# Two half-buffers that each carry four whole batches, at a shift, in a two-layer attention kernel on one core

## The reference

```
def half_ffn(x):                      # layer 0, before and after attention
    x = x + 0.5 * (gelu(LN(x) @ U1 @ V1 + b1) @ U2 @ V2 + b2)
def attn0(x):                         # 16 heads of 8, causal, softmax
    p = softmax(mask(q @ k.T / sqrt(8)));  return LN(p @ v) * gamma + beta @ Wo
def moe(x):                           # layer 1, before and after attention, halved
    shared = silu(x @ sw1) * (x @ sw3) @ sw2
    routed = sum over the 2 best of 8 experts of gate * (gelu(x @ ew1[e]) @ ew2[e])
def attn1(x):                         # 16 heads, features of 16, values of 64, causal
    w = mask(1 + s + s*s/2)           # s = q.k/4, a Taylor series of exp
    return (w @ v) / sum(w) @ Wo
layer: x -> + ffn/2 -> + attn(LN(x)) -> + ffn/2
```

## Time and profile before

| | us |
|---|---|
| median of 3 runs (range) | 1528.44 (1524.53 to 1531.28) |
| the profiled execution's own time | 1527.06 |
| its span, first to last instruction | 1525.3 |
| mean granted TensorE clock | 0.937 of full |
| PE / VectorE (DVE) / ScalarE (ACT) / GpSimd (POOL) busy | 1249.5 / 1078.3 / 757.7 / 307.8 |

### The profile page before, as it was taken

How to read it: one execution, slowest core, us unless ns; L and a number is a source line. 1 busy time by engine, 2 the same in 40 slices (tenths; PEclk the granted TensorE clock), 3 DMA queues, 4 the chain that set the end, 5 groups by cost and what they waited for, 6 DMA issues and landing times. The chain is left out here.

```text
span 1525.3 us, 30378 instructions
## 1 busy us (share of the span) xinstructions
PE 1249.5 (82%) x10040; PEld 687.8 (45%) x10064; DVE 1078.3 (71%) x3235; ACT 757.7 (50%) x1251; POOL 307.8 (20%) x807
## 2 busy tenths in 40 slices
PE   5598659888798877888789887888778889898886
PEld 3254235445443454435454344543445335554544
DVE  6985378667786678856788657876687667776756
ACT  3166336652566435664266532765327663454442
POOL 1024001430014200242002420123101331022220
PEclk8799779998899988999889997999979999999999
DMA  3100000000010000100001000010000100101000
GB/s 114 42 2 1 7 21 22 23 8 22 10 37 7 8 26 6 43 2 11 27 2 43 8 10 21 2 43 8 17 13 1 43 1 2 43 8 43 1 2 14
DMA packets 37243, 29.20 MB, mean 19 GB/s; under 512 B 7960, under 2 KB 36304, under 8 KB 37072
## 3 DMA queue, kind: packets, MB, share of 16 engines
q1 hardware_dynamic: 37072, 27.04, 6.6%
HBM read 5.90 MB, written 2.10 MB: 5 GB/s over the span
## 5 line engine op out<-in xcount | busy, mean ns | idle before, releaser
L772 ACT ACTIVATE left<-bank 128x512 f32<-128x512 f32 x280 | 160.6, 601 | 86.3 <-PE bank L1242 83.8
L814 ACT ACTIVATE right<-bank 128x512 f32<-128x512 f32 x280 | 158.6, 602 | 88.5 <-PE bank L1329 81.5
L962 DVE TENSOR_REDUCE left<-bank 128x4 f32<-128x512 f32 x280 | 184.5, 682 | 22.0 <-PE bank L1223 21.0
L1221 PE MATMUL bank<-left 128*128 128x512 f16 (+1 forms) x448 | 130.2, 341 | 67.0 <-DVE left L952 29.9
L1165 PE MATMUL bank<-right,pairs 128*128 128x512 f16 x588 | 167.9, 410 | 20.1 <-DVE right L1041 11.9
L1092 DVE TENSOR_SCALAR right<-right 128x1024 f32<-128x1024 f32 x168 | 105.7, 655 | 64.9 <-ACT right L814 63.7
L1062 DVE SCALAR_TENSOR_TENSOR right<-bank,right 128x128 f32<-128x128 f32 x448 | 125.9, 343 | 30.2 <-PE bank L1305 26.1
L1355 PE MATMUL bank<-right 128*32 128x256 f32 (+3 forms) x1792 | 133.1, 435 | 0.0
L1305 PE MATMUL bank<-ew,right 128*128 128x128 f32 x896 | 119.7, 278 | 10.0 <-ACT right L791 5.7
L1305 PEld LDWEIGHTS bank<-ew,right 128*128 128x128 f32 x896 | 113.4, 191 | 30.5 <-ACT right L791 11.2
L1242 PE MATMUL bank<-left 128*128 128x512 f16 (+1 forms) x448 | 102.4, 304 | 16.8 <-DMA left<-left 8.9
(11 more groups left out here) (281 smaller groups left out, 2289.8 us busy)
## 6 DMA issues: line engine op xcount, KB each, us to landing
right<-right SPq DMA_DIRECT2D x168, 64.0 KB, 2.1
left<-left SPq DMA_DIRECT2D x168, 32.0 KB, 1.9
left<-x_dram SPq DMA_DIRECT2D x7, 256.0 KB, 2.8
out_dram<-right SPq DMA_DIRECT2D x7, 256.0 KB, 2.5
left<-left SPq DMA_DIRECT2D x24, 64.0 KB, 2.1
right<-right SPq DMA_DIRECT2D x24, 32.0 KB, 1.9
wo<-wo_dram SPq DMA_DIRECT2D x1, 512.0 KB, 3.5
ew<-ew_dram SPq DMA_DIRECT2D x1, 512.0 KB, 4.2
```

The lines of the kernel that those rows point to most:

```text
L772: act.activation(h.probs[:, g % 2, u * S:(u + 1) * S], ps[:, :], ACT.Exp).then_inc(h.act, 1)
L814: act.activation(h.wts[:, p % 2, u * S:(u + 1) * S], ps[:, :], ACT.Square, bias=1.0, scale=FEAT ** -0.5).then_inc(h.act, 1)
L962: dve.tensor_reduce(h.bmax[:, u * NT:(u + 1) * NT], ps[:, :].rearrange("p (b k) -> p b k", k=P), AX.X, ALU.max).then_inc(h.dve, 1)
L1221: mm(ps[:, c0:c0 + n_keys], h.q0a[:, g, qt * P:(qt + 1) * P], h.kpad0[:, g * GH + j, 0:n_keys], start=True, stop=False)
```

## The change

- **Sections.** Each half now carries four whole batches, each as attention and then Taylor: left the even ones (A1, B1), right the odd ones (A2, B2). The right starts when the left has got to `exp 13` of its first attention, and keeps that distance. The body holds a whole batch of each half and is written out three times; there is no hardware loop, and all waits are on constants. At the end the left finishes first and the right's last Taylor stream goes on alone from its seventh square.
- **Hand-over.** `take` and its two buffers are gone, since a half's Taylor stream reads the x that its attention stream left. The next x is loaded (`fetch`) after the first expert of the second feed-forward. The result has a buffer of its own.
- **LayerNorm.** The centring moves from VectorE to GpSimd: with shift = -mean * rstd, four `tensor_scalar` (x * rstd + shift), after two small multiplies and one more tiny addition that carries a wait.
- **Taylor weights.** GpSimd masks first, with -1 as fill, then adds one over the whole stretch of 1024 or 512 columns; VectorE has no part in it.
- **Values.** ScalarE evacuates both banks.

```diff
-SECTIONS = {
-    "begin": {"L": listing(("A1", 0, ORDER_A), ("A1", 1, FRONT)), "R": listing(("A2", 0, ORDER_A))},
-    "body": {"L": listing(("A1", 1, BACK), ("A1", 2, FRONT)), "R": listing(("B2", 0, ORDER_B))},
-    "finish": {"L": listing(("A1", B - 2, BACK), ("B1", 0, ORDER_B)),
-               "R": listing(("B2", B - 3, ORDER_B), ("B2", B - 2, ORDER_B))},
-}
-TURNS = B - 3
+    expert.8 fetch expert.9-15 store""")
+
+BATCH = [("A", step) for step in ORDER_A] + [("B", step) for step in ORDER_B]
+LEFT_CUT, RIGHT_CUT = BATCH.index(("A", "exp 13")), BATCH.index(("A", "stat 0"))
+TURNS = B // 2 - 1
+
+
+def span(side, first, last, turn):
+
+    return [(kind + side, turn, step) for kind, step in BATCH[first:last]]
+
+
+def sections(left, right):
+
+    n = len(BATCH)
+    return {
+        "begin": {"L": span("1", 0, left, 0), "R": span("2", 0, right, 0)},
+        "body": {"L": span("1", left, n, 0) + span("1", 0, left, 1), "R": span("2", right, n, 0) + span("2", 0, right, 1)},
+        "finish": {"L": span("1", left, n, TURNS), "R": span("2", right, n, TURNS)},
+    }
+
+
+SECTIONS = sections(LEFT_CUT, RIGHT_CUT)
 
...
     if name == "v1":
-        return [("low", "act"), ("high", "dve")]
+        return [("low", "act"), ("high", "act")]
...
-        def run(eng, fns, engine):
-
-            steps(fns, 0, "begin", engine)
-            with eng.Fori(0, TURNS) as i:
-                steps(fns, i, "body", engine)
-            steps(fns, 0, "finish", engine)
+        def run(eng, fns, engine, enter=None):
+
+            steps(fns, 0, "begin", engine, enter)
+            for i in range(TURNS):
+                steps(fns, i, "body", engine, enter)
+            steps(fns, 0, "finish", engine, enter)
...
                   .then_inc(h.res_free, 16)
 
-            def load_next(h, it, _n, step):
-                if not (isinstance(it, int) and it == 0):
-                    load(h, it, _n, step)
-
-            run(sp, dict(load=load_next, qkv0=qkv0, shift=shift, qk1=qk1, store=store), "sp")
-            sp.wait_ge(B2.res_free, 16 * B)
-            sp.wait_ge(B1.res_free, 16 * 2)
+            def fetch(h, it, _n, step):
+                if isinstance(it, int) and it == TURNS:
+                    return
+                sp.wait_ge(h.moe_added, (it * 2 + 1) * (NE + 1) + 1)
+                load(h.partner, it + 1)
+
+            run(sp, dict(fetch=fetch, qkv0=qkv0, shift=shift, qk1=qk1, store=store), "sp")
+            for h in (B1, B2):
+                sp.wait_ge(h.res_free, 16 * (B // 2 + 1))
...
@@ -673,8 +678,20 @@
             def ln_scale(h, it, k, step):
                 pool.wait_ge(h.mv_ready, it * h.lns + k + 1)
                 pool.tensor_tensor(h.vare[:, :], h.mv[:, :, 1], epsilon[:, :], ALU.add).then_inc(h.vare_ready, 1)
+                pool.tensor_tensor(h.shift[:, :], h.mv[:, :, 0], minus[:, :], ALU.mult)
                 pool.wait_ge(h.vare_ready, it * h.lns + k + 1)
                 pool.tensor_tensor(h.rstd[:, :], h.vare[:, :], neghalf[:, :], ALU.pow).then_inc(h.rstd_ready, 1)
+                pool.wait_ge(h.rstd_ready, it * h.lns + k + 1)
+                pool.tensor_tensor(h.shift[:, :], h.shift[:, :], h.rstd[:, :], ALU.mult).then_inc(h.shift_ready, 1)
+                pool.wait_ge(h.shift_ready, it * h.lns + k + 1)
+                pool.tensor_tensor(h.spare[:, :], neghalf[0:1, 0:1], neghalf[0:1, 0:1], ALU.add)
+                src = h.attn if h in (A1, A2) and k == 2 else h.x
+                for t in range(NT):
+                    last = pool.tensor_scalar(h.ln[:, t, :], src[:, t, :], h.rstd[:, t:t + 1], h.shift[:, t:t + 1],
+                                              ALU.mult, ALU.add)
+                last.then_inc(h.ln_ready, 1)
+                if h in (A1, A2) and k == 0:
+                    pool.memset(h.vaug[:, :, :, HD0:HD0 + 1], 1.0).then_inc(h.ones_laid, 1)
 
             def wait_apart(h, it, n, sem, value):
 
...
                     k = p * NC + list(COMPLETE1).index(u)
-                    wait_apart(h, it, k, h.plus1, it * NPAIR * NC + k + 1)
-                for kt in COMPLETE1.get(u, ()):
-                    mask(h.wts[:, p % 2, :], 2, kt).then_inc(h.masked1, 1)
+                    wait_apart(h, it, 2 * k, h.act, drained(h, it, step, "s"))
+                    for kt in COMPLETE1[u]:
+                        last = mask(h.wts[:, p % 2, :], 2, kt, -1.0)
+                    last.then_inc(h.cut1, 1)
+                    wait_apart(h, it, 2 * k + 1, h.cut1, it * NPAIR * NC + k + 1)
+                    v = h.wts[:, p % 2, (u // 2 * 2) * S:(u + 1) * S]
+                    pool.tensor_scalar(v, v, 1.0, 1.0, ALU.mult, ALU.add).then_inc(h.masked1, 1)
 
             run(pool, dict(stat=ln_scale, exp=exp, sq=sq), "pool")
 
...
@@ -799,9 +820,9 @@
 
             def values1(h, it, t, step):
                 ps = full(act, h, it, step, "low")
-                if t == NT - 1:
-                    act.wait_ge(h.res_free, 16 * (it + 1))
                 act.activation(h.v1[:, t, 0:S], ps[:, :], ACT.Copy).then_inc(h.act, 1)
+                ps = full(act, h, it, step, "high")
+                act.activation(h.v1[:, t, S:2 * S], ps[:, :], ACT.Copy).then_inc(h.act, 1)
 
             def sq(h, it, n, step):
                 p, u = divmod(n, NU1)
...
@@ -862,10 +883,7 @@
                     dve.wait_ge(h.dve, drained(h, it, *before))
                 elif k == 0:
                     h.chain.start(it, 0)
-                    if h is B1:
-                        dve.wait_ge(last_taken, 1)
-                    else:
-                        dve.wait_ge(mid_taken, it + 1)
+                    dve.wait_ge(h.partner.dve, drained(h.partner, it, "down0 3", "y"))
                 elif k == 1:
                     dve.wait_ge(h.moe_added, (it * 2 + 1) * (NE + 1))
                 else:
...
-            def centre(h, it, k, step):
-
-                src = h.attn if h in (A1, A2) and k == 2 else h.x
-                dve.wait_ge(h.rstd_ready, it * h.lns + k + 1)
-                for t in range(NT):
-                    last = dve.tensor_scalar(h.ln[:, t, :], src[:, t, :], h.mv[:, t, 0:1], h.rstd[:, t:t + 1],
-                                             ALU.subtract, ALU.mult)
-                last.then_inc(h.ln_ready, 1)
 
             def low(h, it, n, step):
                 if h is A1 and isinstance(it, int) and it == 0 and n == 0:
...
                 last.then_inc(h.kpad1_ready, 1)
-
-            def sq(h, it, n, step):
-                p, u = divmod(n, NU1)
-                if u not in COMPLETE1:
-                    return
-                dve.wait_ge(h.act, drained(h, it, step, "s"))
-                v = h.wts[:, p % 2, (u // 2 * 2) * S:(u + 1) * S]
...
```

233 lines of the change are left out of this document (105 added, 128 removed).

## The result

The changed kernel takes 1538.15 us (median of 11 runs, 1528.76 to 1549.94) against 1528.15 us (11 runs, 1523.77 to 1534.11) of the kernel before on the same chip: a ratio of 1.0067, interval 1.0044 to 1.0091. It is slower by 0.7%, where 1483 us was forecast. The profiled execution took 1537.31 us, with a span of 1535.4 us.

A forecast was written before the change was run, and what follows sets the result against it. PE's work plus its idle time was taken as the bound. Start 78, middle 1322 and end 94 make 1494; loop -5, relief -32 and norm +25 give 1482, with 1.8 outside the span about 1483 us; range 1435 to 1552.

The forecast's parts named there:

- Start: Left half alone, before the right starts: 78 us, with 33 us of PE work.
- The middle: Both halves running: 1147.5 us of PE work at a share of 0.868, from halved thin time, giving 1322 us.
- thin stretches: Times when both halves are in dependent steps at once; PE's share there 0.55, their part of time forecast to halve to 0.108.
- the thin stretches only move: Rival for the middle: feed-forwards still face pads and LayerNorms, only the branch goes; share 0.842, 1530 us, chance 0.11.
- VectorE's relief: About 220 us of work leaves VectorE, shortening queues ahead of what PE waits for: -32 us, bounds 0 and -80.
- End: Right half alone, from seven pairs of heads to the last window: 94 us, with 69 us of PE work.
- The loop: PE's 2.48 us idle behind the branch, four times, 10.0 us in all, goes; counted half: -5 us.
- ScalarE: 32 more evacuations of values, 19 us on ScalarE, hidden by its idle time: 0, at most 19 us.
- The norm on GpSimd: Centring in 56 LayerNorms: each chain 0.9 us longer, half of it exposed: +25 us, bounds 0 and 50.
- Additions on GpSimd: Plus one of the Taylor weights, 1.08 us for 1024 columns, covered by the other half's work: cost 0.
- GpSimd's chains: Rival: long additions of 2.2 us make GpSimd's chains the new wait, slower at about 1575 us; chance 0.19.
- What would show it: Signs: middle share near 0.87, centring waits about 70 us; wrong if share under 0.85 or waits on GpSimd over 100 us.

The follow-up runs named there:

- b_noadd: The kernel before with its loop written out, and the plus one of the Taylor weights left out, which VectorE did there: 1503.52 us, ratio 0.9822.
- a_longer: The changed kernel with one more 128-column centring instruction, into a spare tile, on GpSimd in each norm: 1574.08 us, ratio 1.0281 to the kernel before.
- a_centre_dve: The changed kernel with the centring put back on VectorE, its steps given new places in VectorE's order: 1570.51 us, ratio 1.0291 to the kernel before.

## Why the prediction was wrong, point by point

**Start.** Right: 78 us, with 40 us of PE work where 33 was taken.

**The middle** is the step that failed most: the share of 0.868, made of 0.108 x 0.55 + 0.892 x 0.907. With the three further terms (-5, -32, +25) it stood for 1147.5 us of work in 1310, a share of 0.876; measured is 0.833 over the whole middle and 0.842 in its full turns. The first half of the product held: long thin stretches shrank from 12% to 3% of the time, more than halved. What failed is the other half, that the dense stretches keep their share: they went from 0.88 to 0.85, in 10 us windows. In these dense windows PE waits longer for the centring (3.6 us in 100, before 1.3) and for ScalarE (4.4 for 2.5). Of the waits for the centring in the middle, 15 of 26 us fell into thin windows before, and 7 of 44 now. So the waits for the norms moved out of the thin stretches and into the dense ones, where the forecast had allowed for them only with its +25. Whether the shift alone would have done this is not shown. That the 0.842 is the very figure of the rival *the thin stretches only move* is chance: the rival set that share before its -32 and +25, and the thin stretches did more than move. Its 1530 us came nearest of all, but the mechanism behind it is not what the windows show. (A body holds one batch in each half, not two as the prediction says; its sums don't use this. And 1482 + 1.8 is 1484, not 1483.)

**What the single runs add up to.** Loop -13; the norm's chain +31 to +43 (0.58 us on 56 norms, at 0.95 to 1.3); additions on GpSimd +13. Together they make +31 to +43, and +10 was measured over the kernel before. So the new shift and VectorE's relief together gave -21 to -33, with the intervals some 10 us either way, where the forecast had (1494 - 1525) - 32 = -63. At b_noadd's rate the relief of 185.5 us is worth -25, and -8 to +4 is left for the shift; but that rate is a bound from above, and if the relief were worth nothing, the shift would be worth -21 to -33, which holds the forecast's -31. This is a sum, not a run: no kernel here has the new shift alone with orders that fit it, and what the shift is worth by itself stays open.

**End.** Wrong in length: 114 us for 94. PE has 88.6 us of work in it, not 69, and idles 25.5 us there as forecast; the right simply lags by more. It took work out of the middle rather than adding waits. The stretch just ahead of it, which the forecast did not treat apart, is the thinnest of the middle (0.795).

**The loop.** Its size was off: -13 for -5. The 10.0 us of issue idle were not halved by lying in a thin stretch, and something beside them went too.

**VectorE's relief.** At most -25 for -32, from b_noadd's rate. VectorE is busy for 892.8 us, not near 860: its 256 pads, stretched beside GpSimd, take 18 us more than before. The queue in front of the pads and maxima did shrink (PE waits 15.1 us for pads where it waited 32.1, 20.9 for maxima where it waited 26.8), but the wait for the last maximum of a group rose from 4.9 to 27.4 us. The forecast asked which queue grows shorter, not which wait ends last next.

**ScalarE.** Forecast at 0. No run separates the values. PE's waits on ScalarE rose from 44.7 to 69.0 us, on squares, exps and the first feed-forward, so it may not have been free. The new shift, which also changes what stands beside what on ScalarE, is a rival cause that no run excludes.

**The norm on GpSimd.** This term was mis-sized: +25 for +31 to +43. Two errors went against each other. The chain grew by 0.58 us a norm, not 0.9 (means of the 56: the four centrings +0.47, from the power to them +0.24, ahead of the power's end -0.13). The four centrings together, forecast at 1.1 us on either engine, took 1.31 us on VectorE and 1.77 on GpSimd. PE's waits for it came to 69.2 us, where "about 70" was forecast and stood for +23. So the 70 came out right by luck. What was missed is that added waits can cost twice, as in a_longer. I priced PE's idle time alone and held its 1249.5 us of work fixed, though the windows show a clock of 0.74 in a thin stretch. In the sum of the whole change this does not show: PE is busy for 1247.6 us, and the clock rose from 0.937 to 0.945, so all of the miss against 1483 is idle time of PE.

**Additions on GpSimd.** 1.035 us against 1.08; forecast 0, measured 13. The prediction's estimate of 1.45 us took a factor that the Trainium skill (GPSIMD Engine Reference, Engine selection) gives for operations of two inputs, and this one reads one; it takes 1.40 times VectorE's 0.74 us. The rival *GpSimd's chains* did not decide through them: its point was 1.6 us an addition. It was right that waits on GpSimd would be what makes the kernel slower, by another route.

**What would show it.** "Wrong if the share in the middle is under 0.85" is what happened: it was 0.842 at best. PE's waits on GpSimd were 70.5 us, under the 100 named. Watching PE's waits on one engine would not have given the alarm; its share of the middle did.

## What to carry to other kernels

In a kernel whose matmul engine is busy for four fifths, price a longer dependent chain at its whole length and then look at the clock: here 0.58 us on 56 LayerNorms was worth 31 to 43 us by the rates of the single runs, although only 40% of GpSimd and 58% of VectorE were busy. Spreading chains so that they no longer coincide does not hide them by itself: thin stretches fell from 12% to 3% of the time, and the dense ones gave the gain back. Relief of an engine that is not the bound was worth little here (at most 0.13 us per us), and moving its work onto a slower engine on the chain lost. Where orders are written out by hand for one placement, move work only together with the orders, and weigh a move by runs that keep every order, such as one instruction more in the chain or one less.

## What the runs showed of the hardware

*GpSimd's price follows the form of an instruction.* 128 columns of fp32 took 438 to 458 ns as multiply-add or add-multiply with two column scalars, 784 to 804 ns as subtract-multiply with the mean's column. Whether the subtraction is slow or that column, which lies in a tile of means and variances in turn, these runs don't tell apart. Nor did the price of a mask carry over to 128 columns: 0.28 us was drawn from it, 0.44 came. For 1024 columns it did, 1.08 against 1.035.

*GpSimd's masks and long additions hold some of VectorE's instructions, its small operations of four columns don't.* In the changed kernel VectorE's pads took on average 1.9 to 2.9 times their lower quartile when they overlapped a mask or a long addition, 1.1 times beside GpSimd's centring, and 1.0 times beside its operations of four columns, the power among them. Its conversions and some operations of two inputs from SBUF to SBUF were stretched too. The statistics of the norms, from SBUF to SBUF as well, took at most 1.2 times, and what reads PSUM at most 1.1 times. The timeline of VectorE in the changed kernel, four pads of a group whose lower quartile is 340 ns, and that of GpSimd:

```profile
565.14 2.24 DVE L1066 TENSOR_SCALAR left<-left,pairmask 96x512 f16<-96x512 f16 x4 [2.02 <-DMA left<-left]
```

```profile
565.32 0.22 POOL L701 TENSOR_TENSOR spareA<-neghalf 1x1 f32<-1x1 f32 x1 [3.10 <-ACT right L793]
565.50 1.21 POOL L708 TENSOR_SCALAR_AFFINE_SELECT right<-right 128x512 f32<-128x512 f32 x2
```

One pad started 0.08 us ahead of the two masks and took 1.44 us, until 0.15 us after their end. What VectorE's instructions from SBUF to SBUF took above their lower quartiles came to about 41 us in the changed kernel and to 78 in a_centre_dve, where the centring is on VectorE and the additions on GpSimd. In the kernel before it was already 42 us, so in sum the change added none of it. Only the pads met more of it, 29 us for 11. The Trainium skill (GPSIMD Engine Reference, Specifications) has the two engines share interfaces when VectorE is in a 2-port mode or reads two SBUF inputs; the pads and the centring read one, so if it is this, it is the mode.
